# Dispatch scatters gated step by step, results three tiles behind, side products behind values, and down products three steps behind in a macaron layer

## The reference, cut to what matters

```python
# x: (16, 512, 128), E = 8 experts, top_k = 2, d_ff = 512 (128 of it in the shared expert), 16 heads of 8
x = x + 0.5 * ffn(layernorm(x))
x = x + attention(layernorm(x))
x = x + 0.5 * ffn(layernorm(x))

def ffn(x):
    normed = layernorm(x) * gamma + beta
    probs = softmax(normed @ router_w.T)
    top_v, top_i = top_k(probs, 2)
    gates = softmax(top_v)
    out = sum over e of comb[:, e] * swiglu(normed, gate_up_w[e], down_w[e])   # comb: gates at top_i, else 0
    return out + swiglu(normed, shared_gate_up_w, shared_down_w)

def attention(x):
    qk = q @ k / sqrt(8) + q @ rel_emb[r - l + 255]
    return (softmax(qk) @ v) @ Wo.T + bo
```

## Time and profile before

| | |
|---|---|
| three runs | 2271.9, 2274.42, 2279.68 us, median 2274.42 |
| profiled execution | 2267.75 us, its span 2265.8 us |
| TensorE busy | 2055.6 us, 91% |
| VectorE busy | 1849.0 us, 82% |
| ScalarE busy | 1351.1 us, 60% |
| GpSimd busy | 1336.5 us, 59% |
| HBM | 66 GB/s over the span |

### The profile page before, as it was taken

The page is one execution under the profiler, slowest core; times in us unless marked ns, Lnnn a source line. Parts: engine busy times, 40 slices in busy tenths (PEclk is TensorE's granted clock), DMA queues, the critical chain, the costliest instruction groups (busy, mean ns, idle before and its releaser), DMA issues. The chain is left out here.

```text
span 2265.8 us, 64247 instructions
## 1 busy us (share of the span) xinstructions
PE 2055.6 (91%) x22864; PEld 1244.0 (55%) x22865; DVE 1849.0 (82%) x3842; ACT 1351.1 (60%) x3301; POOL 1336.5 (59%) x1961
## 2 busy tenths in 40 slices
PE   7664988996799999999999999999999997889968
PEld 4443988893344444444444444444444447889965
DVE  6543755667699999999999999999999995666648
ACT  4332544556766766666677667667666655445545
POOL 3665155553355557757757667667577583465554
PEclk8666999999999999999999999999999999999989
DMA  5222242217801111210111011012102104232226
GB/s 158 75 67 84 64 151 88 73 50 232 209 13 34 34 26 19 45 34 13 43 34 45 11 38 49 4 39 48 34 12 44 40 24 156 60 89 74 68 63 185
DMA packets 161414, 149.02 MB, mean 66 GB/s; under 512 B 51602, under 2 KB 135698, under 8 KB 160594
## 3 DMA queue, kind: packets, MB, share of 16 engines
q1 hardware_dynamic: 141984, 109.36, 18.6%
q0 software_dynamic: 17280, 35.56, 4.8%
q10 hardware_dynamic: 1874, 0.51, 0.1%
HBM read 86.76 MB, written 62.55 MB: 66 GB/s over the span
## 5 line engine op out<-in xcount | busy, mean ns | idle before, releaser
L1521 PE MATMUL ps_scores<-c_relw,arena_stats 64*64 64x512 f32 x4096 | 956.5, 598 | 0.0
L1972 ACT ACTIVATE arena_probs<-ps_scores,neg_max 128x512 f32<-128x512 f32 x1024 | 697.0, 684 | 393.6 <-DVE neg_max L1857 389.7
L1857 DVE TENSOR_REDUCE neg_max<-ps_scores 128x1 f32<-128x512 f32 x1024 | 650.0, 662 | 26.9 <-PE ps_scores L1521 24.6
L1509 PE MATMUL ps_scores<-arena_rows,arena_stats 64*64 64x512 f32 x2048 | 483.6, 598 | 5.6 <-ACT arena_probs L1972 3.7
L1509 PE MATMUL ps_scores<-c_batch,arena_stats 64*64 64x512 f32 x2048 | 475.3, 596 | 4.7 <-POOL arena_stats L1449 2.6
L1521 PEld LDWEIGHTS ps_scores<-c_relw,arena_stats 64*64 64x64 f32 x4096 | 277.0, 132 | 247.3 <-issue 185.1
L1654 DVE STREAM_TRANSPOSE arena_weights<-arena_probs 128x1024 f32<-128x1024 f32 x256 | 313.5, 1224 | 1.8 <-ACT arena_probs L1972 1.8
L1654 DVE STREAM_TRANSPOSE arena_results<-arena_probs 128x1024 f32<-128x1024 f32 x256 | 313.2, 1224 | 0.0
L1447 POOL TENSOR_TENSOR arena_stats<-arena_rows,c_mask 128x128 f32<-128x128 f32 x256 | 121.9, 476 | 193.2 <-PE ps_scores L1521 191.6
L1447 POOL TENSOR_TENSOR arena_stats<-c_batch,c_mask 128x128 f32<-128x128 f32 x256 | 121.5, 475 | 193.5 <-PE ps_scores L1521 192.3
L1421 POOL DMA_INDIRECT expert_out<-arena_results,f2x_to x142 | 139.4, 982 | 120.8 <-PE ps_scores L1577 73.7
(11 more groups left out here) (323 smaller groups left out, 4225.9 us busy)
## 6 DMA issues: line engine op xcount, KB each, us to landing
qkv_record<-f1c_rec SPq DMA_DIRECT2D x16, 768.0 KB, 3.9
c_batch<-dispatched SPq DMA_DIRECT2D x71, 129.0 KB
arena_rows<-dispatched SPq DMA_DIRECT2D x71, 129.0 KB
c_batch<-qkv_record SPq DMA_DIRECT2D x32, 256.0 KB
arena_rows<-qkv_record SPq DMA_DIRECT2D x32, 256.0 KB
f2c_Y<-expert_out SPq DMA_DIRECT2D x28, 256.0 KB, 3.3
c_Os<-expert_out SPq DMA_DIRECT2D x20, 256.0 KB, 4.1
f1c_Y<-expert_out SPq DMA_DIRECT2D x16, 256.0 KB, 4.3
```

Of the source, the lines that this page charges most:

```text
L1509: m = nc.tensor.matmul(out, SK[n // 2 % NS][p, h, :, :].rearrange("p h a -> p (h a)"), KT[q][p, h, :], start=True, stop=False)
L1521: m = nc.tensor.matmul(out, SR[n // 2 % NS][p, h, :, :].rearrange("p h a -> p (h a)"), R[p, w0:w0 + L], start=False, stop=True)
L1857: reduce_max(nmx[U % NPAIR][:, n % 2:n % 2 + 1], psS[U % NPAIR][n % 2][:], AX, negate=True).then_inc(s_mx, 1)
L1972: nc.scalar.activation(Pr[s][:, n % 2, :], psS[s][n % 2][:], ACT.Exp, bias=nmx[s][:, n % 2:n % 2 + 1], accum_out=rs[:, G % 2, tt:tt + 1]). ...
```

## The change

Six edits. (1) POOL's dispatch scatters of a pair wait, two scatters apart, for the next pair's transposes, logits, best experts (`s_D`), ranks (`s_rk`) and row numbers (`s_E`). (2) The first tile loop has lag 3 throughout. (3) In attention the projection stands one tile later, the transposes and the logits one earlier, the root and what it feeds two earlier. (4) In the second loop the last pair's sends stand in two of three tiles. (5) The semaphores of the second loop's results outlive `attention`; the waits for them and the four early loads go from its end into `finish`. (6) In `finish` all four columns are normalised on ACT, and the down products and what follows stand three batches behind gate and up, with four buffers for `h`.

```diff
-AT_O, AT_ADD, AT_STATS, AT_AGGR, AT_ROOT, AT_ROWS, AT_COPY = 28, 38, 38, 40, 50, 48, 52
-AT_TURN, AT_LOGITS, AT_TOP, AT_EXP, AT_PICK, AT_RANK, AT_PLACE, AT_SEND = 54, 58, 62, 63, 64, 82, 86, 96
+AT_O, AT_ADD, AT_STATS, AT_AGGR, AT_ROOT, AT_ROWS, AT_COPY = 29, 38, 38, 40, 48, 46, 50
+AT_TURN, AT_LOGITS, AT_TOP, AT_EXP, AT_PICK, AT_RANK, AT_PLACE, AT_SEND = 53, 57, 62, 63, 64, 82, 86, 96
...
-                    if s % 2 == 1 and p + 1 < PAIRS:
-                        wait(pool, (s_tp, s + 2))
                     for j in range(JT):
+                        at = JT * (s % 2) + j
+                        if p + 1 < PAIRS:
+                            if at == 1:
+                                wait(pool, (s_tp, 2 * p + 3))
+                            elif at == 2:
+                                wait(pool, (s_lg, 2 * p + 4))
+                            elif at == 3:
+                                wait(pool, (s_D, KD * (p + 2)))
+                        if 0 < p and p + 1 < PAIRS:
+                            if at == 4:
+                                wait(pool, (s_rk, p + 2))
+                            elif at in (5, 6):
+                                wait(pool, (s_E, KE * (p + 1) + KE // 2 * (at - 4)))
                         for k in range(TOPK):
                             t = JT * s + j
-                            if k == 0 and s % 2 == 1 and j == JT // 2 and p + 1 < PAIRS:
-                                wait(pool, (s_lg, s + 3))
...
-                q, y, lag = n % 4, n % YR, max(3, 15 - n // 4)
+                q, y = n % 4, n % YR
...
-                        pool.wait_ge(x_gu, min(ET, n + lag))
+                        pool.wait_ge(x_gu, min(ET, n + 3))
                     else:
-                        pool.wait_ge(s_tx, min(ET, n + lag + 2))
+                        pool.wait_ge(s_tx, min(ET, n + 5))
...
-            for q in range(4):
-                sp.wait_ge(s_st[q], 16 * NG2 * ((ET - q + 3) // 4))
-            yv = yd[0:TOPK * TOK, :].rearrange("(k n p) d -> p k n d", k=TOPK, p=P)
-            for s in range(2):
-                for k in range(TOPK):
-                    sp.dma_start(R2["Y"][s][k], yv[:, k, tokens(s), :]).then_inc(R2["s_ga"][s], 16)
...
-                        if 0 <= n - LATE < TOPK * JP:
-                            send(LASTP, n - LATE)
+                        at = n - LATE
+                        if at >= 0 and at % 3 < 2 and at // 3 * 2 + at % 3 < TOPK * JP:
+                            send(LASTP, at // 3 * 2 + at % 3)
...
-            for q in range(4):
-                pool.wait_ge(s_st[q], 16 * NG2 * ((ET - q + 3) // 4))
...
-            for s in range(2, 5):
+            for q in range(4):
+                sp.wait_ge(s_rows[q], 16 * ROWS * ((ET - q + 3) // 4))
+            for s in range(5):
...
-            for s in range(2):
-                normalize(s)
-            for s in range(NB + 1):
-                if s + 2 < NB:
-                    normalize(s + 2)
-                if s < NB:
-                    hidden(s)
-                    gated(s)
-                if s >= 1:
-                    shared(s - 1)
+            for s in range(AHEAD_H):
+                hidden(s)
+            for s in range(NB):
+                gated(s)
+                if s + AHEAD_H < NB:
+                    hidden(s + AHEAD_H)
+                shared(s)
...
-                if s >= 1:
-                    b = s - 1
+                if s >= AHEAD_H:
+                    b = s - AHEAD_H
```

43 lines of the change are left out of this document (21 added, 22 removed).

## The result

The kernel with the change took 2259.05 us (median of four, 2258.65 to 2260.21), the kernel before 2276.82 (median of four on the same chip). The ratio is 0.9925 with an interval of 0.9904 to 0.9946: faster by 17.8 us, where 57 had been forecast, and 4 us above the range.

The account below looks back on a forecast made before the run. Late signals beside back-to-back scatters were taken to slow dispatch and the first loop, DVE to bound attention and, with PE, `finish`. 17 + 20 + 10 + 3 + 7 = 57 us off 2267.75, plus 6.67 for the median, gave 2217; range 2194 to 2255.

Parts of the forecast that it names:

- A: Dispatch: gates every second scatter let late signals through, a pair takes 21.0 instead of 24.0 us; 17 us, bounds 3 to 25.
- B: First tile loop: lag 3 throughout gives the second loop's constant pace; 20 us, bounds 12 to 23.
- C: Attention: moved inserts remove half of DVE's 21 us of stalls; nothing charged for the root's move; 10 us.
- D: Second loop: sends in two of three tiles, a free tile lets signals catch up; 3 us, bounds 0 to 16.
- E: End and `finish`: POOL's drain starts 1.5 us earlier and DVE has less work in `finish`; 7 us, bounds 0 to 12.
- Count, not order: Rival, chance 0.13: lateness goes by how many scatters POOL issues, not its pauses; A 3, B 8, D 0, so 2246.
- Pauses feed the chain, in turn: Rival, chance 0.05: dispatch's next chain moves only while POOL stands, a pair takes 35 us, so 2312.
- Attention gains nothing: Rival, chance 0.15: the joined insert stalls DVE or the moved root delays POOL's expansion; C is -5, so 2232.
- `finish` gives nothing: Rival, chance 0.08: the drain ends when it did and late loads hold the first `gated`; total 50, so 2224.

Follow-up runs that it names:

- r_before: The kernel before, unchanged, profiled on the same chip as the changed one: 2274.51 us, ratio 0.9999.
- r_after: The changed kernel, unchanged, run on the same chip as the kernel before: 2259.61 us, ratio 0.994.
- e1: The changed kernel with the two dispatch waits a pair of the kernel before: 2241.99 us, ratio 0.9874.
- e3: The changed kernel without the dispatch wait for the next pair's best experts: 2249.36 us, ratio 0.9908.
- e4: The changed kernel with three dispatch waits a pair (logits behind 4 scatters, best experts behind 10, row numbers behind 14): 2246.44 us, ratio 0.9903.
- e5: The changed kernel with no dispatch wait for the next pair, and attention's root and its neighbours two tiles later again: 2256.75 us, ratio 0.9903.
- e9: The changed kernel with the old two dispatch waits and a 256-element write by POOL behind each dispatch scatter: 2233.81 us in one execution.
- g2: The changed kernel with the old dispatch waits, a 256-element POOL write behind each dispatch scatter, and `finish` one batch behind: 2222.65 us, ratio 0.9787.
- r pair: The kernel before and the changed kernel, profiled on one chip one behind the other: 2274.51 and 2259.61 us.
- e2: The kernel before with only lag 3 throughout the first tile loop: 2247.68 us, ratio 0.9913.
- e8: The changed kernel with the old dispatch waits, the root back at 50, and `finish` as before but with late first loads: 2256.33 us, ratio 0.9897.
- e6: The changed kernel with POOL's arithmetic in `finish` cut to 4 of 512 elements (output incomplete): 2249.9 us, ratio 0.9875.
- e7: The changed kernel with `finish`'s down products one batch behind gate and up instead of three: 2254.8 us, ratio 0.9901.
- f1: The changed kernel with old dispatch waits, 32-element POOL writes between dispatch scatters, and `finish` one batch behind, on the 2131.66 us chip: 2123.82 us, ratio 0.9956.

## Why the prediction was wrong, point by point

**A is the step that failed:** "With a gate every second scatter POOL stops as soon as the chain falls behind, which lets the signals through; it then runs at 20.2 + about 0.8 us a pair." Forecast 17 us won, measured 6.0 lost (r_before to r_after), and 8.5 lost by the times for the waits alone. The observation was right: signals are late while scatters stand back to back, and come when POOL stops (140.06 again). The inference from it had two holes. First, a stop opens the way for one signal, and what follows it is computed while POOL stands: at the gate for the best experts POOL paid 4.3 us for a chain that had run beside its work. I had that chain's 6.0 us in hand and put the gate 2.5 us behind the one that starts it. Second, a stop spaces nothing; what follows the last one is a burst of sixteen, as before. e1, e3, e4 and e5 speak against a better number or place: fewer, later or no waits give 192 to 207 us of dispatch, and none reaches the 180 or so that 21 us a pair would need. What a pause could not do, the write behind each scatter did in part (e9, g2): POOL's waits went, the lateness did not. Whether the distance did it, or the mere fact that an instruction of POOL's stands between two scatters, no run on such a chip separates.

One sign of A came true without its gain: the first tile began at 203.56, near the 200 named. What the prediction's signs left out was ACT's 27.4 us behind it.

**B was right:** 20 forecast, 17.9 (r pair), 22 by the times of e2 alone, and 22.3 (the two traces shown first) measured; PE 207.57 of 207.57 us busy.

**C was mis-sized:** 10 forecast, 2.4 measured. The waits of the kernel after, 1080 to 1240 us, have the row that answers to the earlier trace rows:

```profile
DVE neg_max L1860 <- PE ps_scores L1524: 1.4, 3, 0.6
```

The waits halved as forecast, to 1.4 us; but I had priced them as if every microsecond of DVE's waiting in those rows shortened a batch. By the tiles' starts a batch became only 0.48 or 0.19 us shorter (78.07 to 77.59, 79.98 to 79.79). And the last batch grew by 2.6 (84.27 to 86.88). There the root stands directly behind the reciprocals, with a send between, on POOL's timeline of the kernel after:

```profile
1827.75 2.93 POOL L1377 TENSOR_TENSOR row_recip<-row_sum,minus_one 128x16 f32<-128x16 f32 x1
1830.76 0.40 POOL L1379 TENSOR_TENSOR recip_spread<-row_recip,c_maskp 128x128 f32<-128x128 f32 x1
1831.33 1.05 POOL L1412 DMA_INDIRECT dispatched<-c_Os,f_idx  x1 [0.17 <-issue]
...
1833.79 1.04 POOL L1399 TENSOR_TENSOR c_rs<-f_ve,minus_half 128x4 f32<-128x4 f32 x1
...
1836.75 0.48 POOL L1452 TENSOR_TENSOR arena_stats<-arena_rows,c_mask 128x128 f32<-128x128 f32 x1
```

DVE's timeline, three microseconds on:

```profile
1839.06 0.69 DVE L1860 TENSOR_REDUCE neg_max<-ps_scores 128x1 f32<-128x512 f32 x1 [1.55 <-PE ps_scores L1524]
1840.73 0.69 DVE L1860 TENSOR_REDUCE neg_max<-ps_scores 128x1 f32<-128x512 f32 x1 [0.97 <-PE ps_scores L1524]
```

This is the cover of the earlier trace rows that I had named and charged at nothing. Moving the root back (e5, e8) mends the last batch (84.39) and costs each of the others but the first 0.5 to 0.65 us, so that attention is 5.7 longer in all: its new place is right, but for one batch.

**D came to nothing:** 3 forecast; in the r pair the second loop lost 0.5, the tiles around the sends gained 1.1. The free tiles let nothing catch up: on these chips a send costs about 1 us in either order.

**E was mis-sized, its `finish` by sign:** 7 forecast. The end gave 2.1, near the 1.5 forecast, though the drain's row grew, as the rows of the block's end at L1171 show:

```profile
L1171 DVEq DRAIN  x1: 264/264/264, 2178.0 to 2178.0; - x1
L1171 POOLq DRAIN  x1: 11205/11205/11205, 2178.1 to 2178.1; - x1
```

It was 8.97 us in the earlier trace rows. Its length misleads: it now starts at 2178.1, while the last scatter ends at 2180.80. From the last scatter's end (2186.63 before) to the drain's it is 8.5 us, and was 10.5. `finish` lost 0.5 to 1.8 instead of gaining 5.5. I took 0.37 us a batch off DVE and left the gated sums as they were, but 48 of them went from 21.1 us to 28. What failed in E is this term, held constant without a reason. Laid beside POOL's records, 30 of the 48 sums of before meet none of POOL's work and take 0.34 us, the other 18 take 0.76; after the change 26 take 0.34 and 22 take 0.96. More of them collide, and each collision is longer; why it is longer is not shown. e6 prices the collisions, 14.8 us of DVE in 40; e7 the three batches ahead, 3 us of `finish`.

The page "SBUF — State Buffer" of the Trainium skill, under "Who interferes with whom", has the rule for this: a DVE instruction with both inputs in SBUF contends with a GpSimd one that reads SBUF. The trace agrees, by 637 against 345 ns. I had noted that the collision stays wherever the sums stand, and yet priced it as no worse than before.

**The rivals.** "Count, not order" came nearest (28 us, 2246), and joined by attention's, which the prediction put above its range at 2261, it lies 2 us from the 2259 measured: it had A and D small. That is luck in part, since it too had A as a gain. Its reason does not hold alone: in e9 the same count of scatters, only spaced, is 17 us faster. "Pauses feed the chain, in turn" has the sign that A took, but A's loss was far smaller: 24.6 us a pair against its 31. A's lower bound of +3 us was argued from the waits only moving; it left out that a gate can hold POOL for a chain it had been hiding. "Attention gains nothing" and "`finish` gives nothing" both held nearly, and I had treated them as exclusive: each was an optimistic midpoint, and four of them stood in one sum.

**What stays open.** Why signals are late. By the page "SBUF — State Buffer" of the Trainium skill, under "Who interferes with whom", PE and ACT "never wait on anyone", which it says of SBUF's ports. ACT was 27.4 us late here and PE was held up too, so by that rule it is not the port that DVE and POOL share; no run tests it. Nor are semaphores alone late: in the last burst of the kernel after, PE's products of one group, which wait for nothing, start 1.4 to 2.2 us apart instead of 0.12:

```profile
209.56 0.28 PE L965 MATMUL f1d_bank<-f1x_Xh,f1x_Tl 128*128 128x256 f32 x1
209.69 0.28 PE L963 MATMUL f1d_bank<-f1x_Xh,f1x_Th 128*128 128x256 f32 x1
...
211.83 0.28 PE L965 MATMUL f1d_bank<-f1x_Xh,f1x_Tl 128*128 128x256 f32 x1 [1.12 <-issue]
213.25 0.28 PE L963 MATMUL f1d_bank<-f1x_Xh,f1x_Th 128*128 128x256 f32 x1 [1.14 <-issue]
215.47 0.37 PE L964 MATMUL f1d_bank<-f1x_Xl,f1x_Th 128*128 128x256 f32 x1 [1.94 <-issue]
```

What these engines and the scatters share is not in the trace. No gap between the 1.27 us of f1, on the chip without lateness, and the 1.46 of e9 was tried, so the best one isn't known; nor why ACT was still 9.5 (e9) and 17.7 us (g2) late with it. That the chip, not the hour or the set, makes the difference rests on one set of four kernels with 22 runs of before, all near 2132. A part of dispatch's gain there may be the clock, 0.84 to 0.89 against 0.70 to 0.80 granted in 20 to 120 us; in the second loop both are at 1.00.

## What to carry to other kernels

Before you gate a busy queue on a chain, find what of the chain now runs beside the queue's work: a gate placed closer than that chain's length turns hidden time into waiting. Where several operations of one kind stand back to back and everything around them is late, test their spacing before their order. Look for the longest delay, not the first one found: here it was ACT's 27.4 us at the first tile, and no term named it. And when a sum has several terms taken halfway between bounds, let some of them fail: here four of five came out below their forecast.

## What the runs showed of the hardware

- On three chips, beside indirect scatters 1.26 us apart (0.96 us each), signals were late: up to 27.4 us from PE to ACT, 11.4 from PE to DVE (183.05 to 194.40 in the kernel before), 1.2 from DVE to itself. PE stood 1.1 to 1.9 us between products that wait for nothing. Spaced by 1.46 us, POOL hardly waited (0 to 3.2 us in 50 to 212 us, against 34.9), but PE to ACT was still up to 17.7 us late.
- On a fourth chip the changed kernel's variants had none of it (0.04 us from PE to ACT), and the kernel before took 2132 us instead of 2270 to 2278: the chip matters more (6%) than every edit here.
- The drain of POOL at the block's end took 8.97 and 11.2 us where the other engines' took 0.12 to 2.5. It ended 10.5 and 8.5 us behind POOL's last scatter, and ended the block both times.
- A gated sum of DVE (128x128, both inputs in SBUF) took 0.34 us where it met none of POOL's work, and 0.76 to 0.96 where it did.
